# The edge stage of a four-layer graph network, rewritten: leak on ScalarE, products on VectorE, denominators on TensorE

## What is computed

```python
def _L3_gnn_ref(x, adj_matrix, weight, att_src, att_dst):
    H = x @ weight.T
    alpha_src = jnp.sum(H * att_src[0], axis=-1)
    alpha_dst = jnp.sum(H * att_dst[0], axis=-1)
    C = alpha_src[None, :] + alpha_dst[:, None]
    Tau = adj_matrix.T * jnp.exp(jnp.maximum(0.2 * C, C))
    att_weights = Tau / jnp.sum(Tau, axis=1, keepdims=True)
    Z = adj_matrix.T * att_weights @ H
    return Z
...
x = _layernorm(x + _L3_gnn_ref(x, adj, L3_gnn_weight, L3_gnn_att_src, L3_gnn_att_dst), axis=-1)
```

## Time and profile before

| | us |
|---|---|
| median of 3 runs | 12283.2 |
| lowest, highest | 12263.35, 12304.86 |
| the profiled execution | 12270.41 |
| its span, first to last instruction | 12268.5 |
| edge stage in it, from 11698.8 to the end | 569.7 |

### The profile page before, as it was taken

The page is one execution under the profiler, slowest core; times in us unless marked ns, Lnnn a source line. Parts: engine busy times, 40 slices in busy tenths (PEclk is TensorE's granted clock), DMA queues, the critical chain, the costliest instruction groups (busy, mean ns, idle before and its releaser), DMA issues. The chain is left out here.

```text
span 12268.5 us, 378176 instructions
## 1 busy us (share of the span) xinstructions
PE 11106.3 (91%) x138208; PEld 5172.6 (42%) x138208; DVE 10190.5 (83%) x10283; ACT 10590.3 (86%) x9603; POOL 8312.7 (68%) x4135
## 2 busy tenths in 40 slices
PE   5759999999999999998999999998999999999743
PEld 4524444444444444444343344433343433444721
DVE  6358888888788888887888888888888888888388
ACT  3259999999899999998999999999999999998022
POOL 0017777777677777777777777777777777777023
PEclk7979999999899999999999999999999999999866
DMA  8773333333433333333333333333333333333522
GB/s 315 234 221 58 58 58 58 58 58 58 84 56 58 58 58 58 58 58 66 75 53 54 51 55 52 54 52 66 73 54 52 54 53 53 54 51 58 171 88 75
DMA packets 432583, 943.30 MB, mean 77 GB/s; under 512 B 100728, under 2 KB 349439, under 8 KB 381471
## 3 DMA queue, kind: packets, MB, share of 16 engines
q1 hardware_dynamic: 432508, 942.28, 39.4%
HBM read 799.88 MB, written 142.00 MB: 77 GB/s over the span
## 5 line engine op out<-in xcount | busy, mean ns | idle before, releaser
L1011 DVE SCALAR_TENSOR_TENSOR a_probs<-ps,a_adj 128x768 f32<-128x768 f32 (+1 forms) x9216 | 8980.5, 1020 | 1357.6 <-PE ps L904 1244.9
L986 POOL TENSOR_TENSOR a_pool_probs<-a_pool_probs,a_adj 128x768 f32<-128x768 f32 (+1 forms) x4096 | 8102.3, 1978 | 2382.1 <-ACT a_pool_probs L961 2382.1
L966 ACT ACTIVATE a_probs<-a_probs 128x1536 f32<-128x1536 f32 (+3 forms) x5120 | 7345.2, 1457 | 230.8 <-DVE a_probs L1011 199.8
L904 PE MATMUL ps<-a_q,a_k 34*128 34x512 f32 (+2 forms) x26624 | 4998.3, 413 | 416.0 <-DVE a_probs L1011 258.5
L921 PE MATMUL ps<-a_probs,a_v 128*9 128x192 f32 (+1 forms) x73728 | 4218.9, 341 | 5.3 <-ACT a_probs L966 4.0
L961 ACT ACTIVATE a_pool_probs<-ps 128x768 f32<-128x768 f32 (+1 forms) x4096 | 3527.3, 861 | 58.4 <-PE ps L904 37.4
L904 PEld LDWEIGHTS ps<-a_q,a_k 34*128 34x128 f32 x26624 | 2213.7, 185 | 3139.0 <-DVE a_probs L1011 1183.3
L921 PEld LDWEIGHTS ps<-a_probs,a_v 128*9 128x9 f32 x73728 | 1741.3, 90 | 1747.3 <-ACT a_probs L966 617.0
L921 PE MATMUL ps<-a_pool_probs,a_v 128*9 128x192 f32 (+1 forms) x32768 | 2222.3, 343 | 0.0
L921 PEld LDWEIGHTS ps<-a_pool_probs,a_v 128*9 128x9 f32 x32768 | 488.8, 88 | 1227.1 <-issue 1221.0
L1259 POOL TENSOR_TENSOR e_both<-e_tau,e_nat 128x3328 f32<-128x3328 f32 (+1 forms) x26 | 194.5, 7481 | 701.2 <-DVE e_tau L1297 701.2
(11 more groups left out here) (172 smaller groups left out, 2415.6 us busy)
## 6 DMA issues: line engine op xcount, KB each, us to landing
a_k<-k_parts SPq DMA_DIRECT2D x2048, 208.0 KB
a_v<-v_ext SPq DMA_DIRECT2D x512, 117.0 KB
adj_t<-tr SPq DMA_DIRECT2D x26, 1664.0 KB, 6.4
g0tile<-adj_t SPq DMA_DIRECT2D x26, 1664.0 KB, 6.9
g2tile<-adj_t SPq DMA_DIRECT2D x26, 1664.0 KB, 6.8
nat<-in_adj SPq DMA_DIRECT2D x25, 1663.5 KB, 10.3
e_nat<-in_adj SPq DMA_DIRECT2D x25, 1663.5 KB, 6.9
a_q<-q_parts SPq DMA_DIRECT2D x2048, 16.0 KB
```

Source lines behind the costliest of these rows:

```text
L904: ins = nc.tensor.matmul(ps[:, slot + begin:slot + end], kt[row:row + SCORE_ROWS, P * j:P * (j + 1)].bitcast(F32R), qt[row:row + SCORE_ROW ...
L966: nc.scalar.activation(both, both, ACT.Exp, scale=2.0).then_inc(sums_exped, 1)
L986: nc.gpsimd.tensor_tensor(probs(k)[:, :, :], probs(k)[:, :, :], adj_c[:, :, j, :], ALU.mult).then_inc(multiplied, 1)
L1011: v.scalar_tensor_tensor(out=probs(k), in0=score(j).rearrange("p (i q) -> p i q", q=P), scalar=SCALE / 2, in1=adj_c[:, :, j, :], op0=ALU.m ...
```

## The change

The leak is written otherwise. Since max(C, 0.2 C) = 0.2 C + 0.8 Relu(C), and the factor exp(0.2 dst) of a column is in its numerator and in its denominator, it is left out of both. ScalarE makes Relu(dst + src) and then Exp(0.8 r + 0.2 src), in place. VectorE has no leak any more.

Both products, `tau` and `both`, are on VectorE. GpSimd has only five small memsets at the start. The block of H is read in place, so that `h_j` and its copies are gone.

The denominators of columns 0 to 3,071 are summed by TensorE: a stationary operand of ones, 32 columns wide, and four column tiles (output partitions 32g to 32g + 31), each with 768 columns of `tau`, added up in PSUM beside the numerators. VectorE adds only the last 256 columns into `den_of`. At the end TensorE transposes the sums (six transposes) and two small matmuls sum the rest.

`nat` has three buffers. All loops are written out. In the preparation the weight is multiplied by the destination vector first (`by_dst`), so that `dst` needs one pass over x transposed and H transposed isn't made. The copies out of PSUM are shared between ScalarE (2,048 columns) and VectorE (1,280 columns), and ScalarE copies `dst`.

```diff
+EDGE_LOADS = 3
+DEN_COLS = 6 * P
+LEAK = 0.2
...
-        nat = [mem.sb(f"e_nat{b}", [P, NP]) for b in range(2)]
+        att, by_dst = mem.sb("e_att", [P, P]), mem.sb("e_by_dst", [P, P])
+        src, low_src = mem.sb("e_src", [P, BLOCKS]), mem.sb("e_low_src", [P, BLOCKS])
+        ones = mem.sb("e_ones", [P, 32])
+        nat = [mem.sb(f"e_nat{b}", [P, NP]) for b in range(EDGE_LOADS)]
...
-        h_t = both[1]
-        z_t = tau[0]
-        h_j = [mem.sb(f"e_h_j{b}", [P, F]) for b in range(2)]
-        den_of = mem.sb("e_den_of", [P, NP])
+        z_t = edge[0]
+        rest = NP - 4 * DEN_COLS
+        den_of = mem.sb("e_den_of", [P, rest])
+        den_rows = mem.sb("e_den_rows", [P, DEN_COLS])
...
+            for i in range(BLOCKS):
+                b = i % EDGE_LOADS
+                if i >= EDGE_LOADS:
+                    sp.wait_ge(both_ready, i - EDGE_LOADS + 1)
+                if i < BLOCKS - 1:
+                    sp.dma_start(nat[b][:, 0:N], regular[i]).then_inc(loaded[b], LOAD)
+                else:
+                    sp.dma_start(nat[b][0:112, 0:N], adj[FULL:FULL + 112]).then_inc(loaded[b], LOAD)
+                    sp.dma_start(nat[b][112:LAST, 0:N], adj[FULL + 112:N]).then_inc(loaded[b], LOAD)
...
+            pe.wait_ge(att_set, 1)
+            pe.wait_ge(w_copied, 1)
+            nc.tensor.matmul(by_dst_ps, w[:, :], att[:, :], start=True, stop=True).then_inc(by_dst_done, 1)
+            pe.wait_ge(x_copied, 2)
...
-            pe.wait_ge(h_copied, 1)
-            columns(w_t[:, :], x_t, ht_done)
-            pe.wait_ge(ht_copied, 1)
-            columns(att[:, :], h_t, dst_done)
+            pe.wait_ge(w_copied, 2)
+            pe.wait_ge(h_copied, 2)
+            for at in range(0, NP, BANK):
+                end = min(at + BANK, NP)
+                ins = nc.tensor.matmul(ps[:, at:end], by_dst[:, :], x_t[:, at:end], start=True, stop=True)
+            ins.then_inc(dst_done, 1)
...
+            for i in range(BLOCKS):
+                rows, begin, end = rows_of[i], i == 0, i == BLOCKS - 1
+                pe.wait_ge(tau_ready, i + 1)
+                for lo, to in ((0, 7 * BANK - NP), (7 * BANK - NP, DEN_COLS)):
+                    for g in range(4):
+                        ins = nc.tensor.matmul(ps[32 * g:32 * (g + 1), NP + lo:NP + to], ones[0:rows, :],
+                                               tau[i % 2][0:rows, DEN_COLS * g + lo:DEN_COLS * g + to],
+                                               start=begin, stop=end, skip_group_check=True)
+                ins.then_inc(summed, 1)
+                pe.wait_ge(both_ready, i + 1)
                 for at in range(0, NP, BANK):
                     to = min(at + BANK, NP)
...
+                    ins = nc.tensor.matmul(ps[:, at:to], h[0:rows, i, :], both[i % 2][0:rows, at:to],
+                                           start=begin and to < NP, stop=end, skip_group_check=True)
+                ins.then_inc(weighed, 1)
+            pe.wait_ge(z_copied, 2)
+            pe.wait_ge(den_copied, 1)
             for i in range(BLOCKS):
                 ins = nc.tensor.transpose(ps[:, P * i:P * (i + 1)], z_t[:, P * i:P * (i + 1)], keep.ident[:, :])
             ins.then_inc(z_turned, 1)
+            for k in range(DEN_COLS // P):
+                nc.tensor.transpose(ps[:, NP + P * k:NP + P * (k + 1)], den_rows[:, P * k:P * (k + 1)], keep.ident[:, :])
+            pe.wait_ge(rest_added, BLOCKS)
+            for k in range(rest // P):
+                ins = nc.tensor.matmul(ps[:, NP + k + 1:NP + k + 2], den_of[:, P * k:P * (k + 1)], keep.ones[:, :],
+                                       start=True, stop=True)
+            ins.then_inc(den_turned, 1)
...
+            act.wait_ge(x_turned, 1)
+            a.activation(x_t[:, 0:half], ps[:, 0:half], ACT.Copy).then_inc(x_copied, 1)
+            act.wait_ge(h_done, 1)
+            flat_h = h[:, :, :].rearrange("p i f -> p (i f)")
+            a.activation(flat_h[:, 0:half], ps[:, 0:half], ACT.Copy).then_inc(h_copied, 1)
+            act.wait_ge(dst_done, 1)
+            a.activation(dst[:, :], ps[:, 0:NP], ACT.Copy).then_inc(dst_copied, 1)
...
-            def logits(t, b):
-                act.wait_ge(tau_ready[b], t)
-                nc.scalar.activation(edge[b][:, :], dst[:, :], ACT.Identity,
-                                     bias=src[:, bass.ds(2 * t + b, 1)]).then_inc(summed[b], 1)
...
+            for i in range(BLOCKS):
+                if i >= 2:
+                    act.wait_ge(tau_ready, i - 1)
+                a.activation(edge[i % 2][:, :], dst[:, :], ACT.Relu, bias=src[:, i:i + 1]).then_inc(cut, 1)
+                act.wait_ge(cut, i + 1)
+                a.activation(edge[i % 2][:, :], edge[i % 2][:, :], ACT.Exp, bias=low_src[:, i:i + 1],
+                             scale=1.0 - LEAK).then_inc(exped, 1)
+            act.wait_ge(weighed, BLOCKS)
+            a.activation(z_t[:, 0:half], ps[:, 0:half], ACT.Copy).then_inc(z_copied, 1)
...
-                nc.gpsimd.tensor_tensor(both[b][0:rows, :], tau[b][0:rows, :], nat[b][0:rows, :],
-                                        ALU.mult).then_inc(both_ready[b], 1)
...
+            for b in range(EDGE_LOADS):
+                nc.gpsimd.memset(nat[b][:, N:NP], 1.0).then_inc(padded, 1)
+            nc.gpsimd.memset(den_of[:, :], 0.0).then_inc(padded, 1)
+            nc.gpsimd.memset(ones[:, :], 1.0).then_inc(padded, 1)
...
+            v.tensor_copy(x_t[:, half:NP], ps[:, half:NP]).then_inc(x_copied, 1)
...
-            v.tensor_copy(w_t[:, :], w_ps).then_inc(x_copied, 1)
...
+            v.tensor_copy(w_t[:, :], w_ps).then_inc(w_copied, 1)
+            dve.wait_ge(by_dst_done, 1)
+            v.tensor_copy(by_dst[:, :], by_dst_ps).then_inc(w_copied, 1)
...
+            v.tensor_copy(flat_h[:, half:NP], ps[:, half:NP]).then_inc(h_copied, 1)
+            dve.wait_ge(h_copied, 2)
...
+            link(v.reduce_sum(src[:, :], sq, AX.X))
+            v.tensor_scalar(low_src[:, :], src[:, :], LEAK, None, ALU.mult).then_inc(src_ready, 1)
...
-                v.tensor_tensor(den_of[0:rows, :], den_of[0:rows, :], tau[b][0:rows, :], ALU.add).then_inc(den_added, 1)
...
-            def leak(t, b):
-                dve.wait_ge(summed[b], t + 1)
-                v.scalar_tensor_tensor(out=edge[b][:, :], in0=edge[b][:, :], scalar=0.2, in1=edge[b][:, :],
-                                       op0=ALU.mult, op1=ALU.max).then_inc(leaky[b], 1)
...
+            dve.wait_ge(padded, EDGE_LOADS + 2)
+            loads = [0] * EDGE_LOADS
+            for i in range(BLOCKS):
+                b, rows = i % 2, rows_of[i]
+                nat_i = nat[i % EDGE_LOADS]
+                loads[i % EDGE_LOADS] += LOAD * (1 + (i == BLOCKS - 1))
+                dve.wait_ge(exped, i + 1)
+                dve.wait_ge(loaded[i % EDGE_LOADS], loads[i % EDGE_LOADS])
+                if i >= 2:
+                    dve.wait_ge(summed, i - 1)
+                v.tensor_tensor(tau[b][0:rows, :], edge[b][0:rows, :], nat_i[0:rows, :], ALU.mult).then_inc(tau_ready, 1)
+                dve.wait_ge(tau_ready, i + 1)
+                if i >= 2:
+                    dve.wait_ge(weighed, i - 1)
+                v.tensor_tensor(both[b][0:rows, :], tau[b][0:rows, :], nat_i[0:rows, :], ALU.mult).then_inc(both_ready, 1)
+                if i >= 1:
+                    dve.wait_ge(rest_added, i)
+                v.tensor_tensor(den_of[0:rows, :], den_of[0:rows, :], tau[b][0:rows, 4 * DEN_COLS:NP], ALU.add
+                                ).then_inc(rest_added, 1)
+            dve.wait_ge(weighed, BLOCKS)
+            dve.wait_ge(summed, BLOCKS)
+            v.tensor_copy(z_t[:, half:NP], ps[:, half:NP]).then_inc(z_copied, 1)
+            v.tensor_copy(den_rows[:, :], ps[:, NP:8 * BANK]).then_inc(den_copied, 1)
+            dve.wait_ge(den_turned, 1)
+            turned = ps[:, NP:8 * BANK].rearrange("p (k c) -> p c k", c=P)[:, 0:P:32, :]
+            link(v.reciprocal(den[:, 0:4 * DEN_COLS // P].rearrange("p (g k) -> p g k", g=4), turned))
+            link(v.reciprocal(den[:, 4 * DEN_COLS // P:BLOCKS], ps[:, NP + 1:NP + 1 + rest // P]))
```

More of the change, by code:

```diff
@@ L1171, in _ @@
         def _(pe):
-            def columns(lhs, rhs, sem):
-                for at in range(0, NP, BANK):
-                    end = min(at + BANK, NP)
-                    ins = nc.tensor.matmul(ps[:, at:end], lhs, rhs[:, at:end], start=True, stop=True)
-                ins.then_inc(sem, 1)
             for i in range(BLOCKS):
@@ L1271, in _ @@
             link = Chain(dve, chain)
[L1272 to L1274 removed]
+            v.tensor_copy(att[:, :], keep.att_dst[:, :].to_broadcast([P, P])).then_inc(att_set, 1)
             dve.wait_ge(x_turned, 1)
[L1276 removed]
+            v.tensor_copy(x_t[:, half:NP], ps[:, half:NP]).then_inc(x_copied, 1)
             dve.wait_ge(w_turned, 1)
[L1278 removed]
```

120 lines of the change are left out of this document (16 added, 104 removed).

## The result

The changed kernel took **11994.9 us** (median of four runs, 11977.3 to 12022.3). The kernel before took 12294.0 us in the same series (four runs, 12263.4 to 12320.0). The ratio is 0.976, with a 95% interval of 0.973 to 0.979. Forecast were 11999.0 us and a range of 11975 to 12040. The profiled execution took 11991.0 us, with a span of 11989.2.

What follows compares the result with a forecast made beforehand. VectorE was taken to bound the loop at 7.6 us a block. First `tau` 19.4 us earlier, loop 259.7 less and end 5.1 less made 284.2 off the 12283.2 median: 11999.0 us, range 11975 to 12040.

Steps and rivals of the forecast that it cites:

- The bound and its cause: Edge loop before: VectorE bounds at 17.9 us a block; its 10.37 us addition stands still while GpSimd works.
- The block: Edge loop, VectorE: `tau` to `both` 3.66, `both` to addition 3.57, addition to next `tau` 0.36, together 7.6 us.
- The cover: Edge loop, ScalarE: two `edge` buffers let it run a block ahead, hiding its 6.05 us behind VectorE's 7.6.
- TensorE: Edge loop: numerators 5.57, denominators 1.29 with tiles side by side, changes of form 0.24; 7.1 us a block, 0.5 under VectorE.
- Rivals 1, 2 and 4: Loop; 1: TensorE bounds slightly, 12024 us, chance 0.13; 2: tiles serial, 12086, 0.04; 4: tiles serial, clock 0.50, 12354, 0.01.
- The clock: Edge loop, TensorE: busy 7.1 of 7.6 us a block, so full clock was taken, with a cold first block.
- Rival 3: Edge loop: TensorE's clock stays at 0.50, tiles side by side; 14.0 us a block, 12161 us in all; chance 0.03.
- The loads: Edge loop: a block's load lands 6.9 us after issue, issued 15.6 us ahead; hidden with 8 us to spare.
- The start: Edge stage up to the first `tau`: at 11734.6 in place of 11754.03, 19.4 us earlier.
- H takes 8.53 as before: Start of the edge stage: TensorE's matmuls for H keep their earlier 8.53 us, ending at 11714.6.
- the `dst` pass is 7.4 us at the clock of the row: Start of the edge stage: TensorE's one pass for `dst` takes 7.4 us; at 1.2 GHz 11, costing 3.6 more.
- The end: Edge stage, last `both` to the division: 16.3 us in place of 21.4, 5.1 us less.

Runs made afterwards that it cites:

- The first experiment: The kernel before with only the second product (`both`) moved from GpSimd to VectorE: edge stage 470.4 us, a block 14.27 us.
- The experiment with the long pause: The changed kernel with the first copy (x transposed) out of PSUM made by VectorE alone, as before the change: edge stage 281.2 us.

## Why the prediction was right

**The bound and its cause.** VectorE bounded the loop because GpSimd's product made its addition stand still. The first experiment takes only that away and the addition falls from 10.37 to 3.62 us.

**The block.** The sum was 3.66 + 3.57 + 0.36 = 7.6; measured 7.53, in the block shown 3.65 + 3.54 + 0.33 = 7.52. Over the stretch this is 195.5 us in place of 197.3. The narrow addition was put at 0.43 and took 0.418.

**ScalarE.** 6.05 us a block were forecast and a wait of 1.5; measured 6.14 and 1.35. Exp with its new bias and scale takes 3.07 us, as Relu does, not the 2.98 of the earlier trace rows. The cover held.

**TensorE.** 7.1 us a block were forecast, 1.29 + 0.24 of them for the denominators and 5.57 for the numerators. Measured 7.21: 1.43 and 5.78. The reading of the earlier trace rows, that the tiles run side by side, was right; one tile costs 3.85 us a block more, and the stage 90. Of the 0.5 us to spare 0.32 were there. The cold first block put TensorE 4.0 us behind, not 3 (2.79 + 8.59 us in place of 1.50 + 5.85), and it had caught up by the eleventh. Rivals 1, 2 and 4 did not come.

**The clock.** It was full from the third block and stayed so through all of TensorE's 0.25 us waits. Rival 3 was nearer in the kernel with GpSimd's product, where TensorE waited 0.9 to 3.8 us a block: mean 0.88.

**The loads.** Hidden as forecast, and with more to spare than it needed: two buffers would have done but for the last block and 0.2 us in the middle.

**The start, mis-sized by 4.5 us.** The step that failed is "H takes 8.53 as before" with "the `dst` pass is 7.4 us at the clock of the row". I kept the durations of matmuls whose clock depends on the pause ahead of them, though the change shortened that pause: 1.76 us in place of the 3.94 of the earlier trace rows. H took 5.97 us, at full clock, which is 2.6 of the 4.5 us, the `dst` pass 5.82, 1.6 more, and the x transposes 4.59 in place of 4.95, the last 0.4. I bounded only the colder side. The experiment with the long pause gave back 1.6 of H's 2.6 us; the remaining 0.9 is open. For the `dst` pass the pause doesn't explain all: behind the same 2.06 us it took 7.51 or 7.52 us in three executions of the twelve that have it and 5.82 in nine. The three are those in which the x transposes at the stage's start took 5.78 us, the longest; in the nine they took 4.37 to 5.76. The runs leave open what decides it. The start is thus a draw: in the eleven executions with the shared copy the first `tau` came 31.1 to 34.2 us after the stage's start, and the 31.3 of the profiled execution lie at the favourable end.

**The end, mis-sized by 1.6 us.** 26 transposes took 4.70 us in place of 5.47, the six more 0.82 in place of the forecast 1.26; that is 1.2 of the 1.6 us.

**The rest of the program.** That the whole came out 4 us from the forecast is in part luck. The stage was 7.8 us shorter than forecast, and the gain was set against a median of 12283.2 us, where before took 12294.0 in the series of the result: from there it would have given 12009.8. In the profiled execution the stage starts at 11711.5, before it was 11698.8, though nothing ahead of it was changed; so the profiles differ by 279.4 us and the medians by 299.1. In the twelve experiments' and the two first profiles this start lies anywhere between 11679.9 and 11726.7. The last series, with before and after in the same rounds, has 12290.1 and 11976.6, a gain of 313.5 against some 291 in the stage. Whether scatter makes all of the 22 us over that is open: of the kernel before only one profiled execution can be cut at these points.
